# Turning later phases' token rows in 32x32 blocks on VectorE, and moving the blocks through HBM

## What is computed

```python
def ffn(x):                                   # hidden 2048, weights w_gate, w_up, w_down
    return (silu(x @ w_gate.T) * (x @ w_up.T)) @ w_down.T
def attn(x):                                  # W 512x512, K = 4
    lam = sigmoid(lam_logit)
    z = x @ W.T
    m_t = lam[k] * m_{t-1} + z_t              # over the tokens, for each decay k
    h = z + sum_k eta[k] * m[..., k]
    return gamma * LN(h) + beta
x = x + 0.5 * ffn(LN(x))
x = x + attn(LN(x))
x = x + 0.5 * ffn(LN(x))
```

## Time and profile before

| | |
|---|---|
| median of 3 runs | 1044.77 us (1044.32 to 1044.99) |
| the profiled execution | 1046.13 us, span 1044.3 us |
| PE busy | 1036.7 us (99%), 4672 matmuls |
| DVE busy | 645.4 us (62%) |
| ACT busy | 362.0 us (35%) |
| POOL busy | 114.7 us (11%) |
| DMA | 217.89 MB, mean 209 GB/s |

### The profile page before, as it was taken

How to read it: one execution, slowest core, us unless ns; L and a number is a source line. 1 busy time by engine, 2 the same in 40 slices (tenths; PEclk the granted TensorE clock), 3 DMA queues, 4 the chain that set the end, 5 groups by cost and what they waited for, 6 DMA issues and landing times.

```text
span 1044.3 us, 12731 instructions
## 1 busy us (share of the span) xinstructions
PE 1036.7 (99%) x4672; PEld 857.6 (82%) x4672; DVE 645.4 (62%) x973; ACT 362.0 (35%) x605; POOL 114.7 (11%) x127
## 2 busy tenths in 40 slices
PE   9999999999999999999999999999999999999998
PEld 8888888887878888888887888888888888888887
DVE  7855666568687777856749877785665333333342
ACT  6644544533333322212523332232243323222311
POOL 3123332110210200010003020001100000000000
PEclk9999999999999999999999999999999999999999
DMA  6588866677666555648645764554666665556266
GB/s 202 225 320 321 307 248 242 223 232 240 237 221 226 182 156 177 201 142 269 206 159 199 243 211 146 181 173 139 220 224 221 207 202 185 181 191 207 81 191 207
DMA packets 61517, 217.89 MB, mean 209 GB/s; under 512 B 6160, under 2 KB 15376, under 8 KB 53776
## 3 DMA queue, kind: packets, MB, share of 16 engines
q1 hardware_dynamic: 60880, 216.03, 61.5%
q10 hardware_dynamic: 576, 1.05, 0.3%
HBM read 170.92 MB, written 46.14 MB: 208 GB/s over the span
## 4 chain that ended last, share of the span: by engine, by line
PE 94%; DVE 3%; DMA 2%; issue 1%; ACT 0%; SPq 0%; DVEq 0%; ACTq 0%
PE ps_a L1397 8%; PE ps_a L1399 7%; PE ps_a L1398 7%; PE ps_b L1397 7%; PE ps_b L1398 7%; PE ps_b L1399 7%; PE ps_d L1399 6%; PE ps_d L1397 6%; PE ps_d L1398 6%; PE ps_c L1397 6%; PE ps_c L1399 6%; PE ps_c L1398 6%; PE aux L1399 3%; PE aux L1398 3%; PE aux L1397 3%; DMA dn<-dn_kept 1%
## 5 line engine op out<-in xcount | busy, mean ns | idle before, releaser
L924 DVE TENSOR_TENSOR tmp<-tmp,ps_c 128x512 f32<-128x512 f32 x59 | 40.4, 685 | 149.7 <-PE ps_c L1399 149.7
L1397 PE MATMUL ps_a<-xt,gu 128*128 128x512 f32 x304 | 118.9, 391 | 0.1
L1399 PE MATMUL ps_a<-xt,gu 128*128 128x512 f32 x304 | 118.3, 389 | 0.0
L1398 PE MATMUL ps_a<-xt,gu 128*128 128x512 f32 x304 | 118.3, 389 | 0.0
L1397 PE MATMUL ps_b<-xt,gu 128*128 128x512 f32 x286 | 112.3, 393 | 0.3 <-ACT tmp L538 0.2
L1398 PE MATMUL ps_b<-xt,gu 128*128 128x512 f32 x286 | 111.4, 389 | 0.0
L1399 PE MATMUL ps_b<-xt,gu 128*128 128x512 f32 x286 | 111.3, 389 | 0.0
L1397 PE MATMUL ps_d<-dn,hid 128*128 128x512 f32 x256 | 99.8, 390 | 0.0
L1399 PE MATMUL ps_d<-dn,hid 128*128 128x512 f32 x256 | 99.6, 389 | 0.0
L1398 PE MATMUL ps_d<-dn,hid 128*128 128x512 f32 x256 | 99.6, 389 | 0.0
L1397 PE MATMUL ps_c<-xt,gu 128*128 128x512 f32 x236 | 92.2, 391 | 0.1
(11 more groups left out here) (203 smaller groups left out, 2031.9 us busy)
## 6 DMA issues: line engine op xcount, KB each, us to landing
dn<-dn_kept SPq DMA_DIRECT2D x112, 512.0 KB, 3.4
gu<-gu_kept SPq DMA_DIRECT2D x46, 1024.0 KB, 5.1
gu<-gu_kept SPq DMA_DIRECT2D x46, 768.0 KB, 5.4
gu_kept<-gu SPq DMA_DIRECT2D x14, 1024.0 KB, 4.2
gu_kept<-gu SPq DMA_DIRECT2D x14, 768.0 KB, 4.2
dn_kept<-dn SPq DMA_DIRECT2D x16, 512.0 KB, 5.1
h_t<-w_ffn_in SPq DMA_DIRECT2D x18, 256.0 KB, 4.7
x_tok<-w_ffn_in SPq DMA_DIRECT2D x18, 256.0 KB, 5.1
```

Source lines behind the costliest of these rows:

```text
L924: dve.tensor_tensor(dst, u3s(si), p5_bank(si)[:, :], ALU.add).then_inc(c22_done, 1)
L1397: pe.matmul(dst, a_hi, b_hi, start=start, stop=False, skip_group_check=chained)
L1398: pe.matmul(dst, a_hi, b_lo, start=False, stop=False, skip_group_check=chained)
L1399: return pe.matmul(dst, a_lo, b_hi, start=False, stop=stop, skip_group_check=chained)
```

## The change

For phases 1 to 3, PE no longer turns rows. DVE turns each normed row in 32x32 blocks, with the blocks laid so that one half of the turn is done inside a group of 32 partitions. ACT stores pairs of such rows to HBM (512 KB), and reads them back, four rows at a time, in four loads of 32 partitions each (256 KB), which moves the blocks to their partitions. The z rows go the same way, and ACT then copies from the landed rows to `h_t`. The turns of phase 0 stay on PE.

```diff
+            def store_x(k, u):
+                act.wait_ge(x_blocks_turned, 8 * (k - 1) + 2 * u + 2)
+                act.dma_start(x_blocks[k, 2 * u:2 * u + 2].rearrange("s p d -> p s d"), x_turn[:, 2 * u:2 * u + 2, :]
+                              ).then_inc(x_blocks_stored[u], 16)
+            def load_x(k, l):
+                if l == 0:
+                    act.wait_ge(lo0_ready, 16 * k)
+                act.wait_ge(x_blocks_stored[2 * l], 16 * k)
+                act.wait_ge(x_blocks_stored[2 * l + 1], 16 * k)
+                for j in range(4):
+                    act.dma_start(tmp[32 * j:32 * j + 32, 4 * l:4 * l + 4, :].rearrange("p s (i n) -> p (s i) n", i=4),
+                                  to_features(x_blocks[k, 4 * l:4 * l + 4], j)).then_inc(x_landed[l], 16)
+            def blocks_x(k, r):
+                dve.wait_ge(row_x_ready, 8 * k + r - 3)
+                dve.transpose(by_block(x_turn[:, r, :], True), by_block(row_x(k, r))).then_inc(x_blocks_turned, 1)
...
+        def to_features(blocks, j):
+            return blocks.rearrange("s (i r) (j n) -> j r (s i) n", i=4, j=4)[j]
...
+            def place_z(p, j):
+                wait(act, zlo_ready, 8 * (p - 1) + (0 if j < 4 else 4))
+                act.wait_ge(z_landed[j // 4], 64 * p)
+                act.copy(h_t[:, j % 4, :].rearrange("p (g t) -> p g t", t=32),
+                         z_land(j // 4)[:, :, j % 4 * 32:j % 4 * 32 + 32]).then_inc(placed_z, 1)
...
                 for m in range(16):
                     if p < PH - 1:
                         k = p + 1
-                        if 2 <= m < 6:
-                            place_x(k, 2 * m - 4)
-                            place_x(k, 2 * m - 3)
-                        if m == 4:
+                        if 1 <= m < 5:
+                            store_x(k, m - 1)
+                        if m in (3, 5):
+                            load_x(k, m // 4)
+                        if m == 5:
                             hi_x(k, B11)
...
                 for m in range(16):
-                    if m == 0:
+                    if m == (4 if p < PH - 1 else 0):
                         for q in range(ST):
                             add_y0(p, q)
                     if p < PH - 1:
-                        if 1 <= m < 5:
-                            norm_x(k, 2 * m - 2)
-                            norm_x(k, 2 * m - 1)
+                        if m < 4:
+                            for r in (2 * m, 2 * m + 1):
+                                norm_x(k, r)
+                                blocks_x(k, r)
...
                 for m in range(HT):
                     down1(p, m)
-                    if p < PH - 1 and 2 <= m < 6:
-                        turn_x(p + 1, 2 * m - 4)
-                        turn_x(p + 1, 2 * m - 3)
```

288 lines of the change are left out of this document (153 added, 135 removed).

## The result

The changed kernel takes 1111.28 us (median of 6 runs, 1106.6 to 1114.0), beside 1044.26 us of the kernel before on the same chip (6 runs): a ratio of 1.064, with a 95% interval of 1.0626 to 1.0655. It is 67 us slower. I had forecast 1040.4 us in a range of 1031 to 1056.

What follows compares the result with a forecast made beforehand. PE, busy 99% of the span, was taken as the bound. Turns -18.5, start -0.4, windows +3.6 and +1.0, first sets +5.8, set 7 +3.3, set 8 +0.8 sum to -4.4: 1044.8 to 1040.4 us, range 1031 to 1056.

Steps and rivals of the forecast that it cites:

- The turns: PE, phases 1 to 3: removing 96 x and 64 z turns, at 0.11 to 0.12 us each, takes off 18.5 us.
- The start: Before PE's first product: without the decays' load ahead of the first weight stage, everything comes 0.4 us earlier.
- Block turns and norms on DVE: DVE: 40 block turns at 0.65 us each; a pair of norms and block turns takes about 2.6 us.
- The second of my signs of an error: DVE: block turns at 1.2 us would show the forecast wrong, the windows then falling behind 2 to 4 us each.
- The windows: Second down-projection, three times: PE stalls about 1.2 us at step 8, +3.6; late last addition and extra weight stores, +1.0.
- I put the store's landing at 18.9: Each window: the fourth x store, queued behind the first load, lands 18.9 us after the window's start on PE.
- T: Start of a window on PE, from which the forecast counts its times; 212.5 us for the first window.
- I cost at nothing: Windows: weight loads land in 3.4 us, issued 5.4 ahead, so 2 us to spare and no cost.
- The first sets: Two phases, set 2: z rows return late for product 1's copy; stall 1.9 plus 1.0 for weight loads, +5.8 in all.
- Set 7 and set 8: Two phases: product 7's copy late behind z block turns, 1.6 us each, +3.3; then last loads and placing copies, +0.8 both.
- Stores land late: Rival, chance 0.20: store landings above 3.8 us cost up to 10 us per us; at 5.0 the time is 1052.
- Loads into 32 partitions are slow: Rival, chance 0.10: such loads use half the ways into memory, landing in about 9 us, not 6.0; time 1057.

## Why the prediction was wrong, step by step

**The turns, right.** 160 matmuls fewer, and without transfers the trace has a span of 1027.1 us: the span before, 1044.3, less 18.5 and 1.0, with 4.5 us of stalls where there were 1.6, is 1027.7. That the price of a turn is its share of the stream and not its listed length held.

**The start, right in sign.** 0.9 us in place of 0.4; the term held only the issue of the decays' load, not what the load did to the landings behind it, nor ACT's part.

**Block turns and norms on DVE, right.** 0.71 listed and 0.64 in the stream, where I took 0.65. Additions at a window's end did not make PE late. The second of my signs of an error, turns of 1.2, did not come.

**The windows, the step that failed.** I wrote 1.2 us each and it was 11.1, 9.7 and 10.9. Two terms were mis-sized. First the landings, "I put the store's landing at 18.9": the fourth store landed at T + 30 (T = 211.3 here). Most of that is the load ahead of it in the queue: I had it land 6.0 us after its first issue, and it took 13.0 (T + 13.2 to T + 26.3). The second store took 5.6 in place of 3.8, and the fourth landed 3.7 us behind the load in place of 1.3. So the fourth store took 13.9 us from its issue at T + 16.1, where I had 4.8. My 3.8 for a store lay below both rows of stores that I had (4.2 and 5.9). Packets of 512 bytes into 32 partitions are part of it (41 ns and not 28), but with loads to all partitions the fourth store still took 9.6 to 11.3 us; the rest is the queue's order and the traffic of the window. Second, the weight loads "I cost at nothing" with 2 us to spare. The same sentence says that the cover is nearly gone when ACT's loads take half of the DMA engines. PE waited 11.2 us for them in seven places, and the run with all waits late, where PE waited 20.7 us for them, shows that this cost can grow as ACT's waits go. I had a condition for the cover and did not ask whether it held: before the change, from 210 to 255 us, SyncE's queue alone had the DMA engines 79% busy, the down weights landed after 3.1 to 6.9 us there and not after 3.4, and PE had waited for one of them already:

```profile
PE ps_a L1397 <- DMA dn<-dn_kept: 1.5, 1, 1.5
```

**The first sets, right in place, too small.** 2.9 forecast, 9.8 measured. The placing copies cost 1.9 (shown by the run without transfers). The rest is landings: 9.0 us for the store and 11.6 from the load's first issue, in place of 3.8 and 6.0, in the burst of weights for sets 2 and 3. I had seen the burst and priced it at 1.0. The activation's silu became a stall of its own because ACT waits for the store in front of it; I had looked only at the copy of product 1.

**Set 7 and set 8.** 2.5 in place of 1.65, and 3.1 and 2.0 in place of 0.4. The first needs no landing and was near; the second is a landing again (11.1 us from the load's first issue in phase 1, in place of 6.0).

**The clock, missing.** Some 21 us of matmuls at half clock behind the stalls are in no term of the sum. They are nearly a third of the loss. 13 of the 18 stalls, those of 2.5 to 7.0 us, have such matmuls behind them and so cost PE more than their length; the other five, of 0.6 to 2.0 us, have none.

**The rivals.** "Stores land late" had the right mechanism with a price of 10 us for each us; the landings in the bad places took 5 to 9 us longer than I had them, which by that price is 50 to 90 us, but I let the case end at 1052. "Loads into 32 partitions are slow" came true as well (14 us). I had weighed them as cases that exclude each other, with one value each. They add, and both rest on one quantity, how busy the DMA engines are. The range left out their sum.

**What stays open.** 2.6 us of the account. A row of issues that took 8.8 us took 2.4 with a quarter of the packets; how many packets a queue holds before an issue must wait was not measured. In the changed kernel the x loads stood in another queue than the weights, and PE waited 11.2 us for weights all the same; how much more the weights were held in the late runs by standing behind x loads in SyncE's own queue was not tested. Of the version for x that would keep the windows free none was found: with late waits and wide loads, which is not a full turn, it was still 24 us slower than before. That none exists is not shown.

## What to carry to other kernels

When a step leaves a saturated engine for a trip through memory, price the landing where it happens: take the busy share of the DMA engines in that stretch, what stands ahead in the same queue, and what is issued beside it, and not the median of a landing elsewhere. An engine that issues transfers and does work that others wait for must not wait for a landing at a fixed place of its order; put the wait where the landing is long past, and put issues one at a time. A gain of this sort was had in the stage that leaves DMA time (the z rows, 2.8 us); where the stage already lives from DMA (the x rows in the windows) none was found.
